# The decoder's part of each step behind the next block's products: reordering TensorE's program in the last stage

## What is computed

```
q    = relu(xn @ wq)                     # xn: normalised tokens
att  = (per head: vk @ q, divided by its last row + 1e-15) @ wp + bias
rate = sigmoid(moe_out @ c2s_w + c2s_b)  # 64 -> 1024
dec  = sigmoid(rate @ dec_w + dec_b)     # 1024 -> 512
out  = x + att + layernorm(dec) * ln_g + ln_b
```

## Time and profile before

| | us |
|---|---|
| median of 3 runs | 1919.45 |
| lowest and highest of them | 1918.13, 1919.85 |
| the profiled execution | 1916.64 |
| its span, first to last instruction | 1914.9 |
| PE busy in the span | 1871.8 |

### The profile page before, as it was taken

One profiled execution on the slowest core, in us unless ns is written; L12 is line 12 of the kernel. 1 busy time (PEld: TensorE's weight loads), 2 busy tenths in 40 slices (PEclk: granted clock), 3 DMA queues, 4 the chain that ended last, 5 costly groups with the idle time before them and its releaser, 6 DMA issues. The chain is left out here.

```text
span 1914.9 us, 24720 instructions
## 1 busy us (share of the span) xinstructions
PE 1871.8 (98%) x8924; PEld 1553.0 (81%) x8924; DVE 1072.7 (56%) x1999; ACT 748.9 (39%) x1265; POOL 382.9 (20%) x422
## 2 busy tenths in 40 slices
PE   7999999999999999999899999999999999999997
PEld 5888888888788888887678878888888888888886
DVE  6555556554542222222798855666666666666666
ACT  4545555554221222112677723333333333333333
POOL 1000000000004444430000042222222333333331
PEclk9999999999999999999999999999999999999999
DMA  5561333432122233330977631222222222222211
GB/s 212 215 263 67 149 126 122 182 135 100 69 88 93 99 118 116 121 115 28 328 235 237 199 108 71 93 93 94 93 93 89 81 85 88 94 83 94 94 50 66
DMA packets 74824, 233.92 MB, mean 122 GB/s; under 512 B 9856, under 2 KB 15952, under 8 KB 68176
## 3 DMA queue, kind: packets, MB, share of 16 engines
q1 hardware_dynamic: 66432, 219.58, 31.9%
q0 software_dynamic: 8272, 12.76, 2.1%
HBM read 151.95 MB, written 80.36 MB: 121 GB/s over the span
## 5 line engine op out<-in xcount | busy, mean ns | idle before, releaser
L108 PE MATMUL AB_E<-xs,enc_h 128*128 128x512 f32 x512 | 207.3, 405 | 0.0
L110 PE MATMUL AB_E<-xs,enc_h 128*128 128x512 f32 x512 | 200.8, 392 | 0.0
L109 PE MATMUL AB_E<-xs,enc_l 128*128 128x512 f32 x512 | 200.3, 391 | 0.0
L1551 PE MATMUL D_D<-dec_h,rateh 128*128 128x512 f32 x512 | 200.1, 391 | 0.0
L1552 PE MATMUL D_D<-dec_l,rateh 128*128 128x512 f32 x512 | 199.8, 390 | 0.0
L1553 PE MATMUL D_D<-dec_h,ratel 128*128 128x512 f32 x512 | 199.3, 389 | 0.0
L1394 POOL DMA_INDIRECT ga<-eo_scratch,idx x64 | 66.4, 1038 | 647.9 <-DVE ratel L1657 465.9
L596 DVE TENSOR_TENSOR spl<-sp_t,sph 128x512 fp32r<-128x512 f32 x128 | 88.6, 693 | 185.2 <-ACT sph L415 185.0
L915 POOL DMA_INDIRECT slots_scratch<-ctok,idx x128 | 123.8, 967 | 239.8 <-DVE v L1046 120.6
L411 ACT ACTIVATE sp_t<-AB_E,cols 128x512 f32<-128x512 f32 x128 | 88.2, 689 | 193.3 <-PE AB_E L110 193.3
L1450 ACT ACTIVATE rate<-D_Y,cols 128x512 f32<-128x512 f32 x128 | 88.1, 688 | 120.7 <-PE D_Y L1532 120.7
(11 more groups left out here) (318 smaller groups left out, 4521.7 us busy)
## 6 DMA issues: line engine op xcount, KB each, us to landing
xs_scratch<-xs SPq DMA_DIRECT2D x16, 2048.0 KB, 8.3
xsd<-xs_scratch SPq DMA_DIRECT2D x16, 2048.0 KB, 7.9
xs<-xs_scratch SPq DMA_DIRECT2D x14, 2048.0 KB, 8.0
wt<-ew_scratch SPq DMA_DIRECT2D x39, 513.0 KB, 3.8
x<-in_x SPq DMA_DIRECT2D x16, 1024.0 KB, 5.3
xd<-in_x SPq DMA_DIRECT2D x16, 1024.0 KB, 5.6
out_y<-out SPq DMA_DIRECT2D x64, 256.0 KB, 2.0
slots_scratch<-zt SPq DMA_DIRECT2D x1, 9984.0 KB
```

Of the source, the lines that this page charges most:

```text
L108: pe.matmul(out, w_hi, x_hi, start=start, stop=False)
L109: pe.matmul(out, w_lo, x_hi, start=False, stop=False)
L110: return pe.matmul(out, w_hi, x_lo, start=False, stop=stop)
L1551: pe.matmul(bD[t][:, :], rateh[:, n % 3, o], T["dec_h"][:, k, :], start=(k == 0), stop=False)
```

## The change

In TensorE's loop the call of `decoder(i, s)` moves from ahead of the attention's part of the step to behind it. In iteration -1, which has no decoder, `decoder_sum()` stays where it was. No other engine's program is touched.

```diff
                     if has_att and s == HC - 1:
                         rates(i + 1, 0)
-                    if has_dec:
-                        decoder(i, s)
-                    elif s == NT - 1:
+                    if not has_dec and s == NT - 1:
                         decoder_sum()
                     if has_att:
                         if s == HC - 2:
                             middle(i + 1)
                         if s < NT:
                             query(i + 1, s)
                         else:
                             attend(i + 1, s - NT)
                         if 1 <= s <= NT:
                             turn(i + 1, s - 1)
+                    if has_dec:
+                        decoder(i, s)
```

## The result

| | before | changed |
|---|---|---|
| median, us (4 runs each) | 1918.99 | 1930.87 |
| lowest and highest | 1918.13, 1919.85 | 1928.42, 1932.12 |
| profiled execution, its span | 1916.64, 1914.9 | 1931.24, 1929.5 |

The ratio is 1.006 with an interval from 1.0043 to 1.0078: slower, by 8.3 to 15.0 us.

The account below looks back on a forecast made before the run. PE, busy 98% of the span and throughout the changed loop, was taken as the bound. Fifteen holds of 1.06 us, 15.9 us with no gain, took the median from 1919.45 to 1935.4 us; range 1929.0 to 1937.9.

Parts of the forecast that it names:

- The bound: Whole changed loop: PE busy for all 740.72 us at granted clock 1.00, so no idle time for a new order to fill.
- The hold in step 6: Transposes of `middle` wait for the tanh to read bank `bY`: 1.06 us in each of 15 iterations, 15.9 us.
- The restart's price: Release of held transposes to the next product: 0.53 us after an ACT copy or 0.47 after DVE, 0.36 without a hold.
- The row of ACT: Profile row where an ACT copy released transposes: next product 0.53 us later, so 1.06 us per step 6; the one taken.
- Weight loads pulled ahead: Skill's rule for PE's queue: restart hidden, a pause would cost 0.89 us, in all 13.4; not used in the sum.
- The parts costed at nothing: Turns, decoder, banks of queries and values, SP and POOL: intervals the same or more to spare, so no cost.
- the end of the loop: Last decoder, needing `ratel`: done at 1881.49 for 1881.65, 0.16 us left; no cost, at worst 0.3 us once.
- The slow stretch behind transposes: Products behind each group of transposes lose 0.10 us; taken as unchanged at 60 turns, within 1.8 us to either side.
- Rival 2: Decoder behind the 60 turns runs without the 0.10 us loss, giving back 6 us: 1929.4 us; chance 0.06.
- Rival 1: Step 6: PE goes on with work behind the held transposes, no pause forms; price 0, 1919.45 us; chance 0.03.
- rival 3: Clock falls in the 15 pauses, 1.5 us lost at each, 22 us more: 1958 us; chance 0.01.
- The level: Whole kernel's forecast median: 1919.45 us before would go to 1935.4, 0.83% slower.

## Why the prediction was right

- *The bound.* PE was full in the loop, so the change could hardly do anything but cost: confirmed. The four loops without a hold all take 763 us, each in its own order.
- *The hold in step 6.* Foretold were 0.89 us to the end of the tanh, 0.53 from there to the next product, 0.36 of it normal: 1.06 a block. In the changed kernel the tanh ends 0.89 us behind the place where the transposes would have started (1880.59 against 1879.47 + 0.227) and the product follows at 0.53 (1881.12). Fifteen times 1.06 is 15.9, and the loop grew by 15.8. The distance from one `middle` to the next, foretold to grow by about 1.06, went from 49.57 us (1819.37 to 1868.94) to 50.62 (1830.11 to 1880.73), by 1.05. The earlier start of each pair, in the kernel before and in the changed one:

```profile
1819.37 0.60 PE L1522 MATMUL D_Y<-ident,mo 128*128 128x128 f32 x4
```

```profile
1830.11 0.63 PE L1522 MATMUL D_Y<-ident,mo 128*128 128x128 f32 x4 [0.87 <-ACT rate L1450]
```

- *The restart's price* was the choice between two rows, an ACT copy that released transposes and a DVE operation. The row of ACT was right to 0.01 us, but not because ACT releases: the last section shows DVE releasing PE as late as ACT does. So the choice of the row was right partly by luck, since the reason given for it doesn't hold; the other row would have given 0.9 us less, still inside the range. Weight loads pulled ahead, the rule that the prediction took from the Trainium skill (TensorE: Matmul & The Clock Gate, "Step-by-step: what each phase is for"), did not shorten the held restart here: by it the loop would have grown by 13.4. The held weight load starts at 1880.70, 0.11 us behind the tanh's end.
- *The parts costed at nothing* (turns, decoder, banks, SP, POOL) were nothing within 0.1 us of loop: `middle` behind attend keeps all of them and takes the time of the kernel before. For the end of the loop 0.16 us were foretold to be left. In the timeline of the changed kernel:

```profile
1895.40 0.69 DVE L1657 TENSOR_TENSOR ratel<-rate,rateh 128x512 fp32r<-128x512 f32 x1 [1.34 <-ACT rateh L1458]
...
1896.14 0.19 PEld L1551 LDWEIGHTS D_D<-dec_h,rateh 128*128 128x128 f32 x1 [0.21 <-DVE ratel L1657]
1896.19 0.45 PE L1551 MATMUL D_D<-dec_h,rateh 128*128 128x512 f32 x1
1896.48 0.39 PE L1552 MATMUL D_D<-dec_l,rateh 128*128 128x512 f32 x1
```

  `ratel` ended at 1896.09, 0.10 us ahead of the product. That was late enough to hold its weight load to 1896.14, so that the next product came 0.29 us behind it in place of 0.227: 0.06 us, once. The margin was smaller than foretold, and the cost stayed under the 0.3 us that the prediction allowed.
- *The slow stretch behind transposes* stayed, as taken. Fourteen products behind a turn, now the decoder's twelve and the rates, in the timeline of PE:

```profile
1851.38 0.48 PE L1551 MATMUL D_D<-dec_h,rateh 128*128 128x512 f32 x1
...
1854.68 0.39 PE L118 MATMUL CD_X<-wq_h,xsd 128*128 128x512 f32 x1
```

  3.30 us, against 3.28 for the pair in the earlier trace rows. Over all sixty turns of the loop, with the starts taken to the nanosecond, the median is 3.30 in both kernels, and all lie between 3.29 and 3.31. Rival 2 didn't come.
- *Rival 1*, work that passes the held transposes, and *rival 3*, the clock, are refuted by the waits and by the granted clock of 1.00 in the loop, the latter also with pauses of 1.5 us. The Trainium skill's advice in "Matmul Optimizations" (Perfetto Trace Analysis) to run matmuls back to back holds here for the idle time itself; the loops with fifteen pauses of 0.9 and of 1.5 us show no loss of clock.
- *The level.* The forecast of 1935.4 was made from a median of three runs plus 15.9. Measured were 1930.87 and then 1933.72, with 11.9 and 16.8 us over the kernel before. The loop's share is the same in both profiles. What is left of each median when its kernel's loop is taken off is 1156.1 us for the kernel before and 1152.1 for the changed one in the first measurement, and 1153.5 to 1155.1 for every kernel in the later ones. So the first measurement was off to both sides, outside the loop; in the profiles the loop's start moved between 1130.2 and 1136.5 us. The prediction's range took in the spread of the runs that it saw, 1.7 us, and this is more. That 1930.87 lies near the lower end of the range comes from this scatter and not from a smaller hold.

## What to carry to other kernels

When a step is moved, look first at what it stood between: a group of products may be the cover of another engine's read of a bank, although neither it nor its own waits have anything to do with that bank. Between two groups of PE that write the same PSUM bank, with a wait for another engine's read of it, this kernel needed as much other work as that read takes with its latency: 1.03 us from the place where the transposes would have started (1879.47 + 0.227) to where they did (1880.73). Two decoder tiles were enough, one was not, and a second bank did as well. Where the engine that bounds the kernel was full, a longer hold was paid one for one (9.8 us for 9.9), so its price could be read from the profile of before: the end of the releasing operation minus the place in the new order, plus the restart of the nearest like row, minus the distance that the two groups have without a hold.

## What the runs showed that was not expected

A release reached PE late or early whichever engine gave it. From the end of the tanh to the first transpose it took 0.14 us (1880.59 to 1880.73), in all fifteen blocks, against 0.05 from DVE's `qn` to the weight load. That looks like ACT against DVE, but in the kernel before DVE releases PE as late, 0.15 us behind its end at 496.33:

```profile
495.64 0.69 DVE L1046 SCALAR_TENSOR_TENSOR v<-AB_E,v 128x512 fp32r<-128x512 f32 x1
...
496.48 0.39 PE L1002 MATMUL B_A<-v,kh 128*128 128x258 f32 x1 [1.96 <-DVE v L1046]
```

What goes with the late ones is a wait that stands as an instruction of its own on PE's sequencer, 51 ns long, just ahead of the weight load. The view by source line shows it for the transposes at 1880.73 in the changed kernel and for the product at 496.48 in the kernel before (`wait` at L56 is the helper that issues such waits):

```profile
L56 PEldq EVENT_SEMAPHORE  x1: 51/51/51, 1880.6 to 1880.6; - x1
```

```profile
L997 PEldq EVENT_SEMAPHORE  x1: 51/51/51, 496.4 to 496.4; - x1
```

In every run here, each hold of PE of more than 0.1 us that DVE or ACT ended took 0.14 to 0.15 us from the release to the start with such an instruction in between, and 0.05 to 0.06 without one. All the holds that ACT ended have it; of those that DVE ended some do and some don't. No experiment moved a wait from one form to the other, so that it makes the difference is not shown.

And the page's idle time understates a short hold: with one decoder tile between, 0.19 us idle stand for 0.37 us lost a block. Idle time counts from the modelled end of the product ahead (1870.91 + 0.39 = 1871.30), while the next product could have started 0.16 us before that end (1871.14).
